# Shared experts of a mixture-of-experts layer computed on two token tiles at a time with stationary weights, on one NeuronCore

## What is computed

```python
# x, ctx: (16, 128, 512)
k = layernorm(x); v = ctx
x = x + wkv(w, u, k, v)              # a recurrence along the 128 tokens of each sequence:
                                     # y_t = (A*p + E*v_t)/(A*q + E), p and q decayed by exp(w)
h = layernorm(x).reshape(2048, 512)
probs = softmax(h @ gate_w.T)        # 8 experts, top 2 of them per token
moe = sum over the two chosen e of probs_e * down_e(silu(gate_e h) * (up_e h))   # inner width 256
sh = down_s(silu(gate_s h) * (up_s h))                                           # inner width 1024
out = x + moe + sigmoid(h @ shared_gate.T) * sh
```

## Time and profile before

| | us |
|---|---|
| median of 3 runs | 567.2 (565.82 to 568.12) |
| the profiled execution, its time | 566.06 |
| its span in the trace | 564.3 |
| PE busy in the span | 486.2 (86%) |
| DVE busy | 421.3 (75%) |
| POOL busy | 345.4 (61%) |
| ACT busy | 275.9 (49%) |

### The profile page before, as it was taken

The page is one execution under the profiler, slowest core; times in us unless marked ns, Lnnn a source line. Parts: engine busy times, 40 slices in busy tenths (PEclk is TensorE's granted clock), DMA queues, the critical chain, the costliest instruction groups (busy, mean ns, idle before and its releaser), DMA issues.

```text
span 564.3 us, 10142 instructions
## 1 busy us (share of the span) xinstructions
PE 486.2 (86%) x2671; PEld 258.5 (46%) x2671; DVE 421.3 (75%) x954; ACT 275.9 (49%) x534; POOL 345.4 (61%) x422
## 2 busy tenths in 40 slices
PE   1116789899999999999999979999999999999970
PEld 1113345345455555454555435445545555555530
DVE  5678987899989899999898867566656656666650
ACT  4848837575573864765837333433333333333310
POOL 5767956857948669588486364334375565555332
PEclk9999989999999999999999999999999999999995
DMA  7970105105213223151101320315576776677453
GB/s 283 415 271 19 38 19 187 57 21 188 76 46 143 77 82 143 38 188 62 52 20 39 105 88 15 113 45 102 101 122 117 141 119 116 110 131 123 69 73 38
DMA packets 25929, 59.14 MB, mean 105 GB/s; under 512 B 6314, under 2 KB 6314, under 8 KB 24338
## 3 DMA queue, kind: packets, MB, share of 16 engines
q0 software_dynamic: 9824, 20.90, 21.3%
q1 hardware_dynamic: 16050, 37.59, 18.5%
HBM read 37.83 MB, written 20.65 MB: 104 GB/s over the span
## 4 chain that ended last, share of the span: by engine, by line
PE 52%; POOL 17%; issue 10%; DVE 9%; DMA 7%; ACT 3%; SPq 1%; POOLq 0%; DVEq 0%; ACTq 0%
PE GU L884 28%; PE DN L899 14%; DMA out<-wall,idsa 5%; POOL wall L445 4%; PE XT L829 3%; PE HT L829 3%; POOL yb L429 2%; POOL nrm L411 2%; POOL nrm L413 2%; DVE wall L1071 2%; POOL wall L424 2%; POOL wall L421 2%; DVE wall L1078 1%; PE YT L829 1%; SPq L366 1%
## 5 line engine op out<-in xcount | busy, mean ns | idle before, releaser
L884 PE MATMUL GU<-wall,xt 128*128 128x512 f16 x768 | 187.0, 384 | 2.1 <-DVE wall L1173 2.0
L899 PE MATMUL DN<-wall,hx 128*128 128x512 f16 (+1 forms) x618 | 150.8, 380 | 7.2 <-DVE hx L1200 4.5
L884 PEld LDWEIGHTS GU<-wall,xt 128*128 128x128 f16 x768 | 74.8, 99 | 70.4 <-issue 3.7
L584 POOL DMA_INDIRECT out<-wall,idsa x39 | 62.0, 1590 | 73.1 <-SPq L370 35.1
L659 ACT ACTIVATE hx<-HT 128x256 f16<-128x256 f32 x103 | 39.0, 379 | 127.4 <-PE HT L829 110.6
L899 PEld LDWEIGHTS DN<-wall,hx 128*128 128x128 f16 x618 | 60.4, 98 | 81.9 <-issue 6.0
L1200 DVE TENSOR_TENSOR hx<-HT,hx 128x256 f16<-128x256 f32 x103 | 43.1, 418 | 64.3 <-ACT hx L659 59.7
L654 ACT ACTIVATE th<-GU,scl 128x256 f32<-128x256 f32 x103 | 48.5, 471 | 80.0 <-PE GU L884 76.1
L884 PE MATMUL GU<-wall,kb 128*128 x240 | 61.4, 379 | 0.2 <-DVE kb L1374 0.2
L884 PE MATMUL GU<-wall,xnb 128*128 x228 | 58.5, 379 | 0.6 <-DVE xnb L1374 0.6
L574 POOL DMA_INDIRECT xb<-xn_rows,idsi x39 | 40.2, 1030 | 30.5 <-DMA out<-xb 16.3
(11 more groups left out here) (163 smaller groups left out, 747.3 us busy)
## 6 DMA issues: line engine op xcount, KB each, us to landing
wall<-wgu SPq DMA_DIRECT2D x12, 1024.0 KB, 9.7
wall<-wd SPq DMA_DIRECT2D x12, 512.0 KB, 10.3
out<-xb SPq DMA_DIRECT2D x20, 256.0 KB
xb<-x SPq DMA_DIRECT2D x16, 256.0 KB, 2.7
cb<-ctx_t SPq DMA_DIRECT2D x16, 256.0 KB
xn_rows<-xnb SPq DMA_DIRECT2D x16, 256.0 KB
xb<-xn_rows,idsi POOLq DMA_INDIRECT x39
out<-wall,idsa POOLq DMA_INDIRECT x39
```

The lines of the kernel that those rows point to most:

```text
L584: pool.indirect_dma_start(out, bass.IndirectOffsetOnAxis(ap=idsa[:, j:j + 1], axis=0), ye[j % RESULTS], None, compute_op=ALU.add).then_inc ...
L884: ins = nc.tensor.matmul(GU[par][:], lhs(xp, c), gate_up(base, wp, c), start=m == 0, stop=m == 3 * HC - 1)
L899: ins = nc.tensor.matmul(DN[:], hx[par][:, hp * IE + c * P:hp * IE + (c + 1) * P], down(base, wp, c), start=start and m == 0, stop=stop an ...
```

## The change

**Units on pairs.** A shared unit now takes 128 inner columns of two tiles. Its stationary operands are blocks of the weights (128x128), the moving operand is xt of both tiles, 256 tokens wide (`xt_pair`; the layout of xt interleaves the two tiles of a pair). 24 matmuls of 256 columns write gate (first half) and up (second half) of GU with inner columns on partitions. That is the layout that the down products need as their stationary operand, so `hidden_t` and the bank HT are gone for shared units: `unit_hi` and `hidden_lo` read th, which `hidden` writes in place. A pair has PU = 8 units, and there are 64 units as before. The slots keep `unit`, `products` and `hidden_t`.

**Order.** LAG is 3: turn i does four units (half a pair) of group j = i - 3, and a pair starts only when both its tiles have x_lo. Tile 3's recurrence and the first four units are written out ahead of the turns. The turns run from i = 4, and three groups (12 units) are left for the tail, which were two (8 units). `y_back(i - 1)` stands inside the first unit of the next turn. The squares of experts fall in turns 4, 6, ... (expert 0's are ahead of the turns), and the last parts of experts 5 and 6 are split in the tail.

**Banks and buffers.** DN is two banks, one per tile of a pair, and used in turn in the slots; both tiles are accumulated together every second turn. There are NB = 8 rows of x; the six gathers take rows of tiles 8 to 13. yb and hb are gone (the quotient is made in place), small arrays of the lists live in cb. The sums of squares take one matmul instead of two.

```diff
-LAG = 2
+LAG = 3
-NB = 6
+NB = 8
-SQUARED_IN = [2] + list(range(3, 2 * E - 2, 2))
+SQUARED_IN = list(range(LAG + 1, 2 * E + 2, 2))
...
-        HT, DN = bank("HT"), bank("DN")
+        DN = [bank("DN0"), bank("DN1")]
+        HT = YT
...
+        def xt_pair(t, lo, c, first=0, n=2):
+            off = (t // 2 % 2) * (4 * H) + lo * (2 * H) + (c * 2 + first) * P
+            return xt[:, off:off + n * P]
...
             def unit_tanh(n, par, row):
                 act.wait_ge(gu, n + 1)
-                wait_from(act, h_rdy, n - 1)
+                wait_from(act, h_lo, n - 1)
...
             def unit_hi(n, par):
-                act.wait_ge(h_t, n + 1)
+                if n < N_EXP:
+                    act.wait_ge(h_rdy, n + 1)
+                else:
+                    act.wait_ge(h_t, n - N_EXP + 1)
                 wait_from(act, dn, n - 1)
-                nc.scalar.activation(hx[par][:, 0:IE], HT[:, 0:IE], ACT.Copy).then_inc(h_hi, 1)
+                nc.scalar.activation(hx[par][:, 0:IE], th[par][:] if n < N_EXP else HT[:, 0:IE],
+                                     ACT.Copy).then_inc(h_hi, 1)
...
+            def shared_products(n, first, last):
+                u = n % PU
+                for m in range(first, last):
+                    g, c, (xp, wp) = m // (3 * HC), m % (3 * HC) // 3, HI_LO[m % 3]
+                    f = g * IE + u % 2 * P
+                    ins = nc.tensor.matmul(GU[n % 2][:, g * 2 * P:(g + 1) * 2 * P],
+                                           gate_up(sh_base(u // 2), wp, c)[:, f:f + P], xt_pair(n // PU * 2, xp, c),
+                                           start=m % (3 * HC) == 0, stop=m % (3 * HC) == 3 * HC - 1)
+                return ins
+
+            def shared_down(n):
+                u, pair = n % PU, n // PU
+                pe.wait_ge(h_lo, n + 1)
...
+                for a in range(2):
+                    if u == 0:
+                        wait_from(pe, dn_free, 2 * pair - 1 + a)
+                    for m, (hp, wp) in enumerate(HI_LO):
+                        ins = nc.tensor.matmul(DN[a][:], hx[n % 2][:, hp * IE + a * P:hp * IE + (a + 1) * P],
+                                               down(sh_base(u // 2), wp, u % 2), start=u == 0 and m == 0,
+                                               stop=u == PU - 1 and m == 2)
...
+            def shared_units(j, beside={}, between={}, beyond={}):
+                pe.wait_ge(x_lo, j // 2 * 2 + 2)
                 for u in range(SU):
...
+                    wait_from(pe, h_rdy, n - 1)
+                    shared_products(n, 0, 6)
+                    for step in between.get(u, ()):
+                        step()
+                    shared_products(n, 6, 12)
+                    if n >= 2:
+                        shared_down(n - 2)
...
+                    shared_products(n, 12, 24).then_inc(gu, 1)
...
             def hidden(n, par, row):
...
-                wait_from(dve, h_t, n - 1)
-                STT(hb[par][:], th[par][:], scale(row, KAPPA), GU[par][:, IE:2 * IE], ALU.mult,
+                STT(th[par][:], th[par][:], scale(row, KAPPA), GU[par][:, IE:2 * IE], ALU.mult,
                     ALU.mult).then_inc(h_rdy, 1)
...
-            turns(turn, LAG)
-            expert_lo(E - 2, 1)
-            expert_lo(E - 2, 2)
-            norm(B - 1, 1, agg2, norm2, xn_rdy)
+            turns(turn, LAG + 1)
             scatter(B - 4)
...
+            norm(B - 1, 1, agg2, norm2, xn_rdy)
+            expert_lo(E - 3, 0)
+            scatter(B - 3)
+            expert_lo(E - 3, 1)
+            expert_lo(E - 3, 2)
+            scales(E, E - 2)
+            scatter(B - 2)
+            scatter(B - 1)
...
+            for k in range(3):
+                expert_lo(E - 2, k)
             scales(E + 1, E - 1)
...
-                    pool.wait_ge(out_st, 16 * (B - GATHERS + j + 1))
+                    pool.wait_ge(out_st, 16 * (B - NB + j + 1))
```

More of the change, by code:

```diff
@@ L141, in build @@
         th = [sb(f"th{i}", [P, IE]) for i in range(2)]
-        hb = [sb(f"hb{i}", [P, IE]) for i in range(2)]
         hx = [sb(f"hx{i}", [P, 2 * IE], F16) for i in range(2)]
@@ L718, in _ @@
             d_square(2)
+            first_norm(2)
             gu_square(3)
+            d_square(3)
             second_norm(0)
-            d_square(3)
             act_hi(0)
+            both_exps(2)
+            for k in range(3):
+                expert_square(0, k)
             shared_gu_hi(0)
-            first_norm(2)
+            second_norm(1)
+            router_out(0)
+            act_hi(1)
             shared_gu_hi(1)
-            both_exps(2)
+            first_norm(3)
+            shared_d_split(0)
+            both_exps(3)
+            unit_tanh(0, 0, SHARED)
             shared_gu_hi(2)
-            shared_d_split(0)
-            first_norm(3)
+            unit_hi(0, 0)
+            unit_tanh(1, 1, SHARED)
+            first_norm(4)
+            router_out(1)
+            shared_d_split(1)
+            unit_hi(1, 1)
+            second_norm(2)
+            unit_tanh(2, 0, SHARED)
+            unit_hi(2, 0)
+            both_exps(4)
+            first_norm(5)
+            unit_tanh(3, 1, SHARED)
+            act_hi(2)
             shared_gu_hi(3)
@@ L733, in turn @@
                 n = j * SU
-                if j is not None and j > 0:
-                    unit_hi(n - 1, 1)
+                unit_hi(n - 1, 1)
                 unit_tanh(n, 0, SHARED)
@@ L889, in hidden_t, with down_products, unit @@
                 pe.wait_ge(h_rdy, n + 1)
-                wait_from(pe, h_lo, n)
-                transposes(HT, hb[par], IC, h_t)
-            def down_products(n, par, base, start, stop, sums):
+                pe.wait_ge(h_lo, n)
+                transposes(HT, th[par], IC, h_t)
+            def down_products(n, par, base, j):
                 pe.wait_ge(h_lo, n + 1)
-                if start:
-                    wait_from(pe, dn_free, sums)
+                pe.wait_ge(dn_free, B + j - 1)
                 for m in range(3 * IC):
                     c, (hp, wp) = m // 3, HI_LO[m % 3]
-                    ins = nc.tensor.matmul(DN[:], hx[par][:, hp * IE + c * P:hp * IE + (c + 1) * P],
-                                           down(base, wp, c), start=start and m == 0, stop=stop and m == 3 * IC - 1)
+                    ins = nc.tensor.matmul(DN[j % 2][:], hx[par][:, hp * IE + c * P:hp * IE + (c + 1) * P],
+                                           down(base, wp, c), start=m == 0, stop=m == 3 * IC - 1)
                 ins.then_inc(dn, 1)
-            def unit(n, par, lhs, base, before, between=None, beyond=None):
+            def unit(n, par, lhs, base, before, between=None):
                 wait_from(pe, h_rdy, n - 1)
@@ L1236, in _ @@
             reciprocals(0, 0, HC)
-            residual_and_stats(0)
+            first_stats(2)
             scan_e(1)
             scan_ev(1)
+            add_now(1)
+            reciprocals(1, 0, 2)
+            residual_and_stats(0)
+            reciprocals(1, 2, 2)
             small_steps(k=1)
-            add_now(1)
-            first_stats(2)
+            keys(2)
             dve.wait_ge(w_hi, 1)
@@ L1246, in _ @@
             act_lo(0)
-            reciprocals(1, 0, HC)
+            residual_and_stats(1)
+            first_stats(3)
+            dve.wait_ge(consts, CONSTS)
             shared_gu_lo(0)
-            first_stats(3)
-            keys(2)
-            shared_gu_lo(1)
-            dve.wait_ge(consts, CONSTS)
+            scan_e(2)
+            act_lo(1)
+            scan_ev(2)
+            add_now(2)
+            keys(3)
+            reciprocals(2, 0, 2)
+            hidden(0, 0, SHARED)
+            shared_gu_lo(1)
+            reciprocals(2, 2, 2)
+            first_stats(4)
+            hidden_lo(0, 0)
+            dve.wait_ge(scale_step, 2 * SCALE_STEPS + 1)
+            nc.vector.tensor_scalar(half_y[:], scale(SHARED, YINV), 0.5, None, ALU.mult).then_inc(half_rdy, 1)
+            dve.wait_ge(half_rdy, 1)
+            small_steps(t=0)
+            hidden(1, 1, SHARED)
+            scan_e(3)
+            scan_ev(3)
+            hidden_lo(1, 1)
+            add_now(3)
+            choices(0)
+            residual_and_stats(2)
+            hidden(2, 0, SHARED)
+            shared_gu_lo(2)
+            reciprocals(3, 0, 2)
+            hidden_lo(2, 0)
+            keys(4)
+            first_stats(5)
+            hidden(3, 1, SHARED)
+            reciprocals(3, 2, 2)
+            act_lo(2)
+            small_steps(1, 0)
             def turn(i, j, sq_e, hi_e, ws_e, lo_e):
                 n = j * SU
-                later = j is not None and j > 0
                 if i == B - 1:
```

374 lines of the change are left out of this document (205 added, 169 removed).

## The result

The changed kernel takes 590.38 us (median of 4 runs, 588.67 to 591.92); the kernel before, timed beside it, took 566.51 us (4 runs, 565.61 to 568.12). The ratio is 1.0417, with a 95% interval of 1.0378 to 1.0457. The forecast was 554 us, with a range of 546 to 566. The kernel became 4% slower where a gain of 2% was forecast.

What follows compares the result with a forecast made beforehand. The prediction took PE to bound nearly every stage behind the start, with DVE close behind in the turns. Its stage terms summed to a 551.9 us span, plus 1.8 outside: 554 us, range 546 to 566.

Steps and rivals of the forecast that it cites:

- the paragraph on DVE and ACT: Shared units' `hidden` and `hidden_lo`: same number and width, no change in time, bounds 0.1 us each way per step.
- the new bound in the turns: Steady turns: with PE down to 17.5 us a turn, DVE sets the pace, at 18.4 us.
- 18.4 a turn: Turns 5 to 14: DVE's 35.52 us per two turns plus 1.14 of remaining waits and hand-offs; 184.0 us in all.
- waits of 0.98 and 0.16: DVE's waits for ACT in two turns, behind expert-weight splits and for tanh; both claimed to go when PE runs ahead.
- Rival C: Turns stay at 18.9 us because ACT's splits hold DVE up whatever PE does; 560 us, chance 0.16.
- the start: Two terms: first four units and tile 3 at 31.5 us (bounds 29.3 and 36), turn 4 at 20.8 us.
- The tail: After turn 15, twelve shared units: PE's work 49.4 us plus 2.6 of waits, 52.0 us.
- rival B: Every shared unit: weight loads no longer hide under 256-column matmuls, 0.048 us each; 612 us, chance 0.09.
- the 25 ns of excess: Shared units' matmuls: the skill page's gap beyond the matmul alone, which would make the time about 579 us.
- the slots: Slots unchanged on PE, less a wait of about 1 us through the second DN bank: 180.4 us.
- the end: Last adds after the slots: slower first adds catch up as before, 19.3 us.
- the start of the first unit: First shared unit, now also needing tile 1's activations, begins at 46.5 us against 44.85; bounds 44.85 and 63.8.

Runs made afterwards that it cites:

- e1: Changed kernel with `hidden_lo` reading one input from PSUM again (product written over the gate half of GU): 583.86 us, 1.0327 of the kernel before.
- e4: Kernel before without the transposes of the shared units' inner activations (down products read untransposed values): 560.63 us, ratio 0.9904.
- e5: e3 with ScalarE's cast after the turn's first expert piece and `hidden_lo` between the two scans, every turn: 570.96 us, 1.0102 of the kernel before.
- e3: e1 with `y_back` of tile 3 one unit later on PE, in the first turn alone: 580.29 us, 1.0263 of the kernel before.
- e6: e5 with the start reordered on ScalarE and VectorE (casts, tanh and `hidden_lo` earlier): 566.74 us, 1.0036 of the kernel before.
- e9: e6 with casts, `hidden_lo` and the accumulates moved earlier in the last three tiles: 565.12 us, 0.9996 of the kernel before.
- e11: Changed kernel with all the reordering of e6, but `hidden_lo` reading both inputs from SBUF: 578.04 us, 1.0221 of the kernel before.

## Why the prediction was wrong

**The step that failed first** stands in the paragraph on DVE and ACT: "that they now read th from SBUF and not a PSUM bank has no row of its own, I take no change, bounds 0.1 us either way for each, 0.4 us a turn." Measured: +0.33 us for each `hidden_lo` on average, up to 2.6 for one, and 21 us of VectorE's time. I bounded the price by 0.1 us a step; what held the step was the product that runs on POOL beside it, 2.14 us long, a row that stood there and was read for POOL's work alone. 16 of the 36.9 us lie in turns 5 to 14; there e1 takes 9.6 off (5 x 1.91). The trace of before held a sign of it that the prediction does not use: its step of 128x2 on DVE, 0.17 us otherwise, lasts 1.06 in three turns, each time beside POOL's quotient.

```profile
189.18 1.31 POOL L429 TENSOR_TENSOR yb<-wall 128x512 f32<-128x512 f32 x1
...
189.46 1.06 DVE L1154 TENSOR_SCALAR chosen<-ix 128x2 f32<-128x2 uint32 x1
```

**The second is the new bound in the turns.** 18.4 a turn came from taking waits of 0.98 and 0.16 off VectorE because PE is relieved. e4 gives PE that relief alone and gets 18.7. e1 stands at 19.2, since PE now waited at each unit for `hidden_lo`. Rival C, turns at 18.9, named the mechanism (ScalarE's splits hold VectorE up whatever PE does), and the remedy, the cast ahead of the pieces, was worth 1.05 us a pair in e5 together with `hidden_lo` between the scans. I had named the wait of 0.98 and costed it as gone; in after a wait for the cast stands there still, in every second turn:

```profile
214.59 0.42 DVE L1313 TENSOR_TENSOR hx<-th,hx 128x256 f16<-128x256 f32 x1 [1.25 <-ACT hx L692]
```

In the series of mended kernels this step weighed more than the hold-up: e5 took 9.3 us off where e1 took 6.5, e3 3.6 and e6 4.2.

**The third is the start**, 11.4 us over in two terms. I summed VectorE's work and added 2 us of waits, without following the order on ScalarE and PE: `first_norm(4)` stands ahead of `unit_hi(1)`, `y_back(3)` ahead of three quarters of unit 4's products. e3 and e6 took 3.6 and 4.2 us back by order alone. Behind the 9.36 us wait PE also ran slowly: six matmuls from 86.43 to 87.71 us, 0.213 each, twice the 0.109, so at 1.2 GHz; the granted clock of that window is 0.83 on average.

**The tail** was 5.6 over. PE's work there was as forecast (50.6 busy, 49.4 forecast); the waits were not, 7.0 us where 2.6 were forecast. e9 took 3.1 us off that stretch against e6, 1.5 of them beyond PE's busy time.

**What held:** rival B's refutation (0.109 us a matmul with its own load; the rule of the Trainium skill in TensorE: Matmul & The Clock Gate, The mechanism, that loads overlap only other row groups, does not describe these rows, nor did the 25 ns of excess from its Back-to-back issue gap come), the slots, the end, the start of the first unit, and that PE loses 14 us of transposes. No rival had the hold-up, and nearly all of my chance for slower was B. The sign is not the hold-up's alone: without it the kernel is still 3.3% slower (e1), with it and the order mended 2.2% (e11), and only with the hold-up gone and the order mended is it even with the kernel before (e9, 0.9996).

Open stays how much of the loss in the changed kernel's own order is the hold-up alone: e1 takes it away only against an earlier wait, since no PSUM bank is free.

## What to carry to other kernels

When a change moves an operand from PSUM to SBUF, count the inputs in SBUF of each VectorE instruction that reads it and look at what POOL runs beside it: here the price went by what was left of POOL's instruction, not by the step's own length. When two engines are both near the pace, price the added side first: here relief of one was worth little (14 us of TensorE's work gave 5.4) and added work on the other was paid in full (15.7 us of VectorE's time cost 19). The longer lag between tiles freed steps to move; the changed kernel had not moved them, and doing so (e5, e6, e9) took 15 us off.
